# Gate and up of a tile gathered into six PSUM groups with one LoRA episode in halves of the array, the down projection a tile later, and a rearranged start

## What is computed

```python
x = x + _L0_cond_ref(x, itok_B_8_3872, log_dt, C, log_A_real, A_imag, D)
...
    def lora_add(base, inp, A, B):
        Ab = A[layer_idx][lora_indices]
        Bb = B[layer_idx][lora_indices]
        t = jnp.einsum('bri,bni->bnr', Ab, inp)
        return base + jnp.einsum('bor,bnr->bno', Bb, t) * SCALE
    gate = lora_add(jnp.einsum('bnh,fh->bnf', x, W_gate), x, A_gate, B_gate)
    up = lora_add(jnp.einsum('bnh,fh->bnf', x, W_up), x, A_up, B_up)
    act = jax.nn.silu(gate) * up
    down = lora_add(jnp.einsum('bnf,hf->bnh', act, W_down), act, A_down, B_down)
x = x + down
```

## Time and profile before

| | |
|---|---|
| median of 3 runs | 526.56 us (526.27 to 527.46) |
| the profiled execution | 526.18 us |
| its span, first to last instruction | 524.4 us |
| TensorE busy | 492.5 us, 94% of the span |
| VectorE, ScalarE, GpSimd busy | 293.3, 198.2, 44.8 us |
| granted TensorE clock | 1.000 of 2.4 GHz |
| DMA | 82.74 MB, 158 GB/s in the mean |

### The profile page before, as it was taken

The page is one execution under the profiler, slowest core; times in us unless marked ns, Lnnn a source line. Parts: engine busy times, 40 slices in busy tenths (PEclk is TensorE's granted clock), DMA queues, the critical chain, the costliest instruction groups (busy, mean ns, idle before and its releaser), DMA issues.

```text
span 524.4 us, 10006 instructions
## 1 busy us (share of the span) xinstructions
PE 492.5 (94%) x2940; PEld 447.3 (85%) x2940; DVE 293.3 (56%) x617; ACT 198.2 (38%) x411; POOL 44.8 (9%) x55
## 2 busy tenths in 40 slices
PE   0099989999999999999999999999999999999997
PEld 0088988899898989898998989898989898989986
DVE  7893258845474646464654645464737374646541
ACT  5790048523343333333333334233424342433330
POOL 1007600100000000000101000010101010101000
PEclk9999999999999999999999999999999999999999
DMA  7799999546574756565556555565646465655520
GB/s 258 281 320 381 368 293 264 111 106 155 102 174 90 176 103 162 117 156 119 152 112 148 121 133 123 138 131 123 146 103 165 91 170 103 161 118 151 108 62 21
DMA packets 175443, 82.74 MB, mean 158 GB/s; under 512 B 128034, under 2 KB 157282, under 8 KB 175426
## 3 DMA queue, kind: packets, MB, share of 16 engines
q1 hardware_dynamic: 175426, 82.54, 61.9%
HBM read 63.46 MB, written 19.04 MB: 157 GB/s over the span
## 4 chain that ended last, share of the span: by engine, by line
PE 90%; DVE 4%; DMA 4%; issue 1%; DVEq 0%; ACT 0%; SPq 0%
PE ps_u L1123 23%; PE ps_g L1123 23%; PE ps_db L1081 13%; PE ps_da L1081 13%; PE ps_g L1047 3%; PE ps_x L1073 3%; DMA toep<-kpad 2%; PE ps_g L1133 2%; PE ps_u L1133 2%; PE ps_u L1134 2%; PE ps_g L1134 2%; PE ps_u L1047 2%; DMA kpad<-k_sb 2%; PE ps_da L1190 1%; PE ps_db L1191 1%
## 5 line engine op out<-in xcount | busy, mean ns | idle before, releaser
L1123 PE MATMUL ps_g<-w_hi,x_hi 128*128 128x512 f32 (+1 forms) x192 | 72.7, 379 | 1.4 <-DVE x_lo L1000 1.4
L1123 PE MATMUL ps_u<-w_lo,x_hi 128*128 128x512 f32 (+1 forms) x192 | 71.4, 372 | 0.0
L1123 PE MATMUL ps_u<-w_hi,x_lo 128*128 128x512 f32 (+1 forms) x192 | 71.4, 372 | 0.0
L1123 PE MATMUL ps_g<-w_hi,x_lo 128*128 128x512 f32 (+1 forms) x192 | 71.4, 372 | 0.0
L1123 PE MATMUL ps_u<-w_hi,x_hi 128*128 128x512 f32 (+1 forms) x192 | 71.4, 372 | 0.0
L1123 PE MATMUL ps_g<-w_lo,x_hi 128*128 128x512 f32 (+1 forms) x192 | 70.9, 369 | 0.0
L879 DVE TENSOR_TENSOR b_spl<-b_raw,b_spl 64x512 fp32r<-64x512 f32 (+1 forms) x96 | 57.9, 629 | 15.3 <-ACT b_spl L527 13.7
L527 ACT CAST b_spl<-b_raw 64x512 fp32r<-64x512 f32 (+1 forms) x96 | 51.8, 571 | 35.7 <-PE ps_u L1134 33.8
L941 DVE TENSOR_TENSOR h_act<-h_act,ps_u 128x512 f32<-128x512 f32 (+1 forms) x48 | 30.3, 632 | 55.2 <-PE ps_u L1134 36.8
L1081 PE MATMUL ps_da<-wd_hi,ht_hi 128*128 128x288 f32 (+1 forms) x176 | 52.1, 296 | 0.0
L1081 PE MATMUL ps_db<-wd_lo,ht_hi 128*128 128x288 f32 (+1 forms) x176 | 51.9, 295 | 0.0
(11 more groups left out here) (170 smaller groups left out, 893.1 us busy)
## 6 DMA issues: line engine op xcount, KB each, us to landing
a_raw<-atab SPq DMA_DIRECT2D x64, 152.0 KB, 2.4
toep<-kpad SPq DMA_DIRECT2D x16, 512.0 KB, 6.4
b_raw<-btab SPq DMA_DIRECT2D x128, 64.0 KB, 2.2
h_raw<-hrow SPq DMA_DIRECT2D x30, 256.0 KB, 2.9
um<-xr SPq DMA_DIRECT2D x16, 256.0 KB, 5.2
x<-xT SPq DMA_DIRECT2D x8, 512.0 KB, 6.9
w_raw<-wgu SPq DMA_DIRECT2D x8, 512.0 KB, 9.6
xrow<-x_sq SPq DMA_DIRECT2D x64, 64.0 KB, 2.2
```

The costliest lines, as they stand in the source:

```text
L1123: T.matmul(ps[:, 0:w], xs[:, kb, :], ws[:, kb, col:col + w], start=(kb == 0 and xs is x_hi and ws is w_hi), stop=False)
```

## The change

TensorE's order in a tile becomes: all six base groups, each in a PSUM bank of its own (`ps_gate`, `ps_up`), with the transpose and the down LoRA of tile t-2 and A of tile t between them; then one LoRA episode for all three chunks; then the whole down projection of tile t-1. In the episode, gate's B stands in partitions 0 to 63 and up's in 64 to 127 (`b_top` and `b_rem` for high part and remainder), t stands once in each half, and three terms of 64 rows are multiplied for each group, gate and up in turn.

On TensorE, a piece of the tile loop before: the end of a base group, the transpose of the masked down LoRA (`td_m`), and the two matmuls of one group's LoRA.

```diff
-NP_POOL = 2 * KB
+NP_POOL = NP_GU
...
-            store_taps(0)
             for pair in range(RC):
                 load_toep(pair, pair, 0)
...
+            magnitudes(1)
+            magnitudes(2)
+            act.wait_ge(k_ready, 1)
+            act.dma_start(taps_rows(0), k_sb[:, 0, :, :]).then_inc(k_out[0], 16)
+            magnitudes(3)
...
                     pool.wait_ge(a_ps, t)
-                    pool.wait_ge(a_in, 16 * BT * (t + 1))
                     pool.wait_ge(x1_ok, PAIRS)
                     nc.gpsimd.tensor_copy(xt[:, :, :].rearrange("p k (h b) -> p k h b", b=BT),
                                           x[:, :, :, bass.ds(t * BT, BT)].rearrange("p h k b -> p k h b")
                                           ).then_inc(xt_ok, 1)
+                    pool.wait_ge(a_in, 16 * BT * (t + 1))
                     pack_a(t)
...
+            def beside(i):
+
+                if i < 6:
+                    half_step(i)
+                    phase_step(0, i)
+                else:
+                    residue_step(2 * i - 12)
+                    residue_step(2 * i - 11)
...
-            q_, s_ = exp_parts(sm(DAR), 0, 1, residue_step)
+            q_, s_ = exp_parts(sm(DAR), 0, 1, beside)
...
+                for c in range(NC):
+                    gated(c)
+                    if c == 2 and k > 0 and not last:
+                        x_lo_part(t + 1)
+                    if last:
+                        ht_lo_part(t, c, True)
+                    else:
+                        square_h(c)
...
+            def lora_b(t, c):
+                c0, w = CH[c]
+                g, u = slice(0, LR), slice(LR, P)
+                for ts, bs, end in ((t_hi, b_top, False), (t_hi, b_rem, False), (t_lo, b_top, True)):
+                    gate = T.matmul(ps_gate[c][:, 0:w], ts[g, :], bs[g, c0:c0 + w], start=False, stop=end)
+                    up = T.matmul(ps_up[c][:, 0:w], ts[u, :], bs[u, c0:c0 + w], start=False, stop=end)
+                gate.then_inc(g_ps, 1)
+                up.then_inc(u_ps, 1)
...
+                base(0, 0)
+                if k > 1:
+                    transpose_td(t - 2)
+                base(0, 1)
+                base(1, 0)
+                if k > 1:
+                    down_lora(t - 2, (ps_da, ps_db))
+                base(1, 1)
+                lora_a(t)
+                base(2, 0)
+                base(2, 1).then_inc(base_ps, 1)
+                pe.wait_ge(tlo_ok, t + 1)
+                pe.wait_ge(b_lo, t + 1)
+                for c in range(NC):
+                    lora_b(t, c)
+                if k > 0:
+                    pe.wait_ge(w_rem_dve, len(pieces) - NP_POOL)
+                    pe.wait_ge(ad_lo, t)
+                    if k > 1:
+                        pe.wait_ge(y_ok, 2 * (t - 1))
+                    for c in range(NC):
+                        down_chunk(t - 1, c)
```

More of the change, by code:

```diff
@@ L451, in _, with body @@
             pack_a(0)
[L453 removed]
+            def body(a, q, k, last):
                 if not last:
@@ new lines, in body @@
+                act.wait_ge(tm_ok, t + 1)
+                nc.scalar.copy(t_hi[:, :], t_m[:, :, :].rearrange("p h b -> p (h b)")).then_inc(thi_ok, 1)
+                if k == 1:
+                    ht_hi_part(t - 1, 1)
+                if k > 0:
+                    bd_hi_part(t - 1)
+                    ht_hi_part(t - 1, 2)
+                if k == 0:
+                    nc.scalar.activation(spare[:, :], t_m[:, 0, 0:1], ACT.Silu)
+                    x_hi_part(t + 1)
+                for c in range(NC):
+                    silu(c)
+                    if last:
+                        turned_hi_part(c)
@@ L619, in td_hi_part @@
+                if k > 0 and not last:
+                    x_hi_part(t + 1)
+                if k == 0:
+                    for n in range(NP_GU + 3, NP_GU + 6):
+                        top_part(n)
+                if k > 0 and not last:
+                    ht_hi_part(t, 0)
+                if k > 0:
+                    ad_hi_part(t)
             def td_hi_part(t):
@@ L646, in chain, with behind, side @@
                 if now:
-                    dve.wait_ge(steps, count[0])
+                    dve.wait_ge(steps, mine)
+            def behind(done, back):
+                if len(done) >= back:
+                    dve.wait_ge(steps, done[-back])
+            def side(ins, done):
+                count[0] += 1
+                ins.then_inc(steps, 1)
+                done.append(count[0])
             def step(ins, now=True):
@@ L998, in first_x_lo @@
+                if k > 0 and not last:
+                    ht_lo_part(t, 0)
+                if k > 0:
+                    ad_lo_part(t)
             def first_x_lo(h0, h1):
@@ new lines, in _ @@
+            tiles(pe, body)
+            end, z = NT - 1, (ps_u[0], ps_u[1])
+            pe.wait_ge(htlo_ok, (NC + 1) * end + 1)
+            for f in range(0, 4):
+                down(f, 0, z)
+            transpose_td(end - 1)
+            pe.wait_ge(htlo_ok, (NC + 1) * end + 2)
+            for f in range(4, 8):
+                down(f, 0, z)
+            down_lora(end - 1, (ps_da, ps_db))
+            pe.wait_ge(ad_lo, NT)
+            for f in range(0, 8):
+                down(f, 1, z)
@@ L1200 @@
+            pe.wait_ge(htlo_ok, (NC + 1) * NT)
+            for f in range(8, FB):
+                ins = down(f, 1, z)
+            ins.then_inc(ad_ps, 1)
+            for f in range(8, FB):
+                ins = down(f, 0, z)
+            ins.then_inc(down_ps, 1)
+            transpose_td(end)
+            down_lora(end, z)
 def kernel(x, itok_B_8_3872, itok_B_2_6, L0_cond_log_dt, L0_cond_C, L0_cond_log_A_real, L0_cond_A_imag, L0_cond_D,
```

691 lines of the change are left out of this document (317 added, 374 removed).

## The result

The changed kernel takes 535.81 us as a median (533.21 to 537.10), the kernel before 526.48 beside it: a ratio of 1.0167, with a 95% interval of 1.0148 to 1.0186. It is slower by 1.7%, where 0.9% faster was forecast. The profiled execution took 534.45, its span is 532.7, which is 8.3 more than the 524.4 of before.

What follows compares the result with a forecast made beforehand. TensorE, busy for 492.5 of 524.4 us, was taken to bound the kernel by its work in a tile and its start. From the median of 526.56, 3.0 (LoRA's B products) and 1.7 (head) gave 521.9; range 514 to 529.

Steps and rivals of the forecast that it cites:

- the part on the down projection: Tile loop: down projection a tile later, six groups in PSUM; claimed to cost nothing, with 2.8 us of cover left.
- A second step: VectorE in a tile: x's squaring and the down LoRA's mask, behind the third squaring, are wanted a tile later; no cost.
- A third: A's product shares a bank with the last up group; its mask must be read out within 1.9 us; no cost.
- The episode: LoRA's B products on TensorE: 2.29 us a tile instead of 2.48, switch included; 3.0 us gained in 16 tiles.
- The cover for `x_lo`: Tile loop: x's remainder is ready at 8.05, wanted at 10.9 by the next base groups; 2.8 us of cover.
- GpSimd's twelve remainders: First tile: remainders and a pack of A end at 79, A's product comes at 82.6; no cost, 3 us of cover.
- the head: Start of the kernel: VectorE's first chains side by side and steps moved into gaps; 1.7 us gained, bounds nothing and 2.6.
- if the transfers swallow it: Lower bound of the head's gain: nothing, if the transfers swallow it; their share is 0.40 from 20 to 25.
- the 3.0: Gain in us forecast for LoRA's B products on TensorE, 0.19 a tile in 16 tiles.
- weights not hidden: Rival in the LoRA episode: each pair waits 0.11 for its weights, 0.71 lost a tile, 536.3 us; chance 0.07.
- prediction's own sign of being wrong: LoRA episode on TensorE: the prediction is wrong where the episode with its switches takes over 2.5 us.
- cover too thin: Rival in the tiles: chain to x_lo takes 3.3 us more than counted, 14 tiles wait 0.5 each, 528.9; chance 0.05.

Runs made afterwards that it cites:

- the loop cut: A's loads put behind the load of h's second piece in SyncE's queue from the second tile on, against the changed kernel: 525.02 us, 0.9979 of the kernel before.
- the one first: Mask of A's product (t_m) put ahead of B's remainder and y's additions on VectorE, against the changed kernel: 532.02 us, 1.0132 of the kernel before.
- with the other: Down LoRA's mask (td_m) put ahead of the third squaring on VectorE, against the changed kernel: 535.47 us, 1.0181 of the kernel before.

## Why the prediction was wrong

**The step that failed** is in the part on the down projection: "SyncE issues 42 DMAs a tile in both; h's loads stand behind B's in its queue and have most of a tile to spare." The count was right and says nothing. What counts is which waits stand in the queue with how much issuing between them. The prices were in the trace of before, in SyncE's queue:

```profile
191.92 2.05 SPq L360 DMA_DIRECT2D hrow<-h_sq  x4
196.71 0.38 SPq L367 DMA_DIRECT2D h_raw<-hrow  x1
```

Four issues take 2.05, 0.5 each, and between the two lines SyncE reads the four indices in 2.7. For 30 issues and four indices that makes some 18; in the changed kernel it is 18.6 from the load of the down projection's B to h's second piece. To these belonged the landing of the piece and ScalarE's and VectorE's work up to the next `bd_spl`, 9.8 (214.21 to 224.04). The sum is 28, more than the 27.6 forecast for a tile. It was never made; no operation in it is long and no engine in it is full.

**A second step** was wrong by itself: what queues behind the third squaring "is wanted a tile later". The mask `td_m` is wanted after the first base group of the next tile, a few microseconds on, and it cost 3.2 in the second tile. There the granted clock made it dearer. Engines' busy time in two stretches (TensorE, its weight loads, VectorE, ScalarE, GpSimd, then the granted clock, DMA share and GB/s):

```profile
120.60:124.20 3.60, 0.44 (x3) 0.07 (x2) 1.43 (x3) 0.00 (x0) 0.00 (x0) 1.00 0.65 125
124.20:128.00 3.80, 3.80 (x12) 3.04 (x13) 1.77 (x3) 1.46 (x3) 0.00 (x0) 0.66 0.82 170
```

TensorE stood for 3.2 us, and in the 3.8 us behind it the mean granted clock was 0.66: part of that stretch ran at 1.2 GHz. This step is not the loop: with the loop cut, the second tile was still 3.7 too long.

**A third** was too short: the mask of A's product "must be read out within one base group", for which 1.9 us were counted, and its own length is small. That VectorE has B's remainder of 1.6 us and y's additions ahead of it, which hang on h's piece, was not counted.

**What held.** The episode: 1.95 and a switch of 0.34 were to make 2.29, and it takes 2.28 (from 280.40, a usual turn behind 280.24, to 282.68, a usual turn ahead of 282.81). Two errors cancel in that: pairs of 352 columns take 0.16 and not 0.19, so the pairs make 1.86, and the switch is 0.4. A tile of 27.6 was forecast; it is 27.52, and where the further 0.1 came from was not traced. The pairs run at once, at the turn of one, with hidden weights. The cover for `x_lo` held in every tile but the second, where 0.8 was missing. GpSimd's twelve remainders were done at 79.45 (79 was forecast with A's pack), and the pack itself took 2.02 (1.04 in the next tile), so its cover shrank from 3 us to about 1, and nothing waited. Of the head, VectorE's part was right, with the first taps at 16.89 instead of 18.98, 2.1 where 1.7 was forecast; the bound "if the transfers swallow it" is what happened to most of it. With the loop cut, 525.0 is left against the 521.9 forecast, near 3: 3.7 in the second tile and about 1.0 that the head missed, less 1.6 that the tiles gained beyond the 3.0.

**A warning on rivals.** The time measured, 535.8, is that of the rival "weights not hidden", 536.3. That is chance. It would have been easy to take the time for the proof. Its own sign, pairs 0.34 apart, is absent from the second pair on. Nor did the prediction's own sign of being wrong, an episode of over 2.5, appear; the one that did is that waits of TensorE stand between tiles. The rival nearest in kind was "cover too thin", which counted one chain once and allowed it 14 waits of 0.5; the true mechanism is that chain's sibling, closed to a loop.

## What to carry to other kernels

When a change gathers work that was spread over a tile, write down for every in-order queue, the DMA-issuing one first, its waits and the issuing between them, and look for a path that returns to its own start one tile later. If its sum exceeds the tile, it is the pace, whatever the engines' busy shares say. In the profile here the loop showed as a share of the chain that left TensorE for a queue, and as waits that changed their names more than their size when a last link was moved: 7.7 us for the two masks in the changed kernel, 7.4 with the one first, 8.4 with the other. The cure was to take issuing out of the loop, not to hurry the link that TensorE meets.

## What the runs showed of the hardware

Two matmuls of 64 rows in different halves of the array took the turn of one of 128 rows, 0.23 for 512 columns, each with weights of its own, and they paired up even where three of one half stood ahead of three of the other in the program. The Trainium skill (TensorE: Matmul & The Clock Gate, The mechanism) calls matmuls strictly first in, first out in start and end; by the records of this case an up matmul starts 0.32 ahead of a gate matmul that stands before it in the program. Whether something between the program and the engine's queue changed their order can't be seen here. A stay in halves cost some 0.4 in all, in four turns of about 0.1, and not in one gap.
